# PV with three fp16 products for all four heads of a group, the fourth split by ScalarE and VectorE

## The reference

```python
h = jnp.maximum(_layernorm(x), 0.0)
q, k, v = (split_heads(h @ W.T) for W in (Wq, Wk, Wv))   # 16 heads, hd = 32
a = einsum('bhnd,bhmd->bhnm', q, k) * 512 ** -0.5 + (adj + adj)[:, None]
p = softmax(where(any(a != 0, -1, keepdims=True), a, -inf)); p = where(isnan(p), 0, p)
o = einsum('bhnm,bhmd->bhnd', p, v)
out = x + o.transpose(0, 2, 1, 3).reshape(B, N, D) @ Wo.T
```

## Time and profile before

| | |
|---|---|
| median of 3 runs | 1099.92 us (1098.54 to 1100.93) |
| profiled execution | 1103.56 us, of which the span from first to last instruction is 1101.7 us |
| mean granted TensorE clock | 0.990 |
| PE busy | 1071.4 us, 97% of the span |
| ACT busy | 923.4 us, 84% |
| DVE busy | 896.1 us, 81% |
| POOL busy | 743.8 us, 68% |
| PV: fp32 products (L1020), 512 records | 135.4 us |
| PV: fp16 products (L1025), 2304 records | 95.2 + 75.3 us |
| DVE's copy of the turned head (L720), 128 | 88.2 us |
| ACT's v_y (L541), 64 | 17.4 us |

### The profile page before, as it was taken

How to read it: one execution, slowest core, us unless ns; L and a number is a source line. 1 busy time by engine, 2 the same in 40 slices (tenths; PEclk the granted TensorE clock), 3 DMA queues, 4 the chain that set the end, 5 groups by cost and what they waited for, 6 DMA issues and landing times.

```text
span 1101.7 us, 34625 instructions
## 1 busy us (share of the span) xinstructions
PE 1071.4 (97%) x11852; PEld 716.0 (65%) x11852; DVE 896.1 (81%) x3218; ACT 923.4 (84%) x3089; POOL 743.8 (68%) x936
## 2 busy tenths in 40 slices
PE   6789999999999999999999999999999999999987
PEld 5556666666766666666666766666766666666643
DVE  6778888888888888888888888888888888888784
ACT  3488888888888888888888888888988888888884
POOL 1266776677767677677667777667776766767665
PEclk9899999999999999999999999999999999999998
DMA  6167887766777776788877788877777868777866
GB/s 229 39 116 144 161 169 150 159 142 148 156 170 160 150 151 141 153 164 167 146 159 145 153 155 166 156 152 145 150 156 167 159 149 164 133 152 140 139 124 143
DMA packets 443118, 165.84 MB, mean 151 GB/s; under 512 B 408128, under 2 KB 416320, under 8 KB 442944
## 3 DMA queue, kind: packets, MB, share of 16 engines
q1 hardware_dynamic: 442944, 163.64, 73.0%
HBM read 46.14 MB, written 16.78 MB: 57 GB/s over the span
## 4 chain that ended last, share of the span: by engine, by line
PE 93%; DVE 2%; POOL 1%; ACT 1%; DMA 1%; issue 1%; POOLq 0%; SPq 0%; DVEq 0%; ACTq 0%
PE ps L955 60%; PE ps L973 9%; PE ps L1025 6%; PE ps L1020 6%; PE ps L986 5%; PE ps L999 4%; PE ps L838 3%; DVE w_max L603 1%; POOL p L400 1%; DMA w_nat<-in_L_gnn_Wq 1%; ACT probs L492 1%; PE ps L1036 1%; PE ps L850 0%; DMA pt<-p 0%; DVE w_lo L643 0%
## 5 line engine op out<-in xcount | busy, mean ns | idle before, releaser
L400 POOL TENSOR_TENSOR p<-probs,p 128x512 f16<-128x512 f32 x384 | 445.3, 1160 | 301.0 <-ACT p L505 301.0
L683 DVE CUSTOM_DVE_ANT_0 logits<-ps,adj_s,sigma 128x256 f32<-128x256 f32 x1024 | 433.3, 479 | 102.7 <-PE ps L973 102.7
L492 ACT ACTIVATE probs<-logits,row_min 128x256 f32<-128x256 f32 x1024 | 506.3, 500 | 1.2 <-DVE row_min L683 0.7
L955 PE MATMUL ps<-ht_hi,w_hi 128*128 128x256 f16 x1024 | 280.4, 274 | 1.6 <-DVE q_lo L736 1.2
L955 PE MATMUL ps<-ht_hi,w_lo 128*128 128x256 f16 x1024 | 279.7, 273 | 0.0
L955 PE MATMUL ps<-ht_lo,w_hi 128*128 128x256 f16 x1024 | 279.7, 273 | 0.0
L505 ACT ACTIVATE p<-probs 128x512 f16<-128x512 f32 x384 | 237.6, 619 | 0.0
L492 ACT ACTIVATION_READ_ACCUMULATOR probs<-logits,row_min 128x1 f32 x1024 | 198.2, 194 | 0.0
L1020 PE MATMUL ps<-probs_t,v_y 128*32 128x256 f32 x512 | 135.4, 387 | 0.0
L955 PEld LDWEIGHTS ps<-ht_hi,w_hi 128*128 128x128 f16 x1024 | 100.3, 98 | 37.0 <-issue 25.3
L720 DVE COPY probs_t<-ps 128x512 f32<-128x512 f32 x128 | 88.2, 689 | 32.5 <-PE ps L986 32.3
(11 more groups left out here) (90 smaller groups left out, 1943.2 us busy)
## 6 DMA issues: line engine op xcount, KB each, us to landing
xs<-in_x SPq DMA_DIRECT2D x32, 512.0 KB, 4.0
x_res<-in_x SPq DMA_DIRECT2D x32, 512.0 KB, 3.9
out<-x_res SPq DMA_DIRECT2D x64, 256.0 KB, 2.4
adj_raw<-in_adj SPq DMA_DIRECT2D x32, 256.0 KB, 4.3
pt<-p SPq DMA_TRANSPOSE x384, 3.1
w_nat<-in_L_gnn_Wq SPq DMA_DIRECT2D x1, 1024.0 KB, 6.0
w_nat<-in_L_gnn_Wk SPq DMA_DIRECT2D x1, 1024.0 KB, 8.3
w_nat<-in_L_gnn_Wv SPq DMA_DIRECT2D x1, 1024.0 KB, 10.5
```

Of the source, the lines that this page charges most:

```text
L400: g.tensor_tensor(p16[:, c % 2, k, 1], probs[:, h % 4].rearrange("p u n -> p (u n)"), p16[:, c % 2, k, 0], ALU.subtract).then_inc(p_split, 1)
L492: e = a.activation(probs[:, h % 4, u, :], logits[:, h % 4, u, :], ACT.Exp, bias=row_min[:, t.par(d), u, h:h + 1], scale=-1.0, accum_out=ro ...
L683: v.tensor_tensor_reduce(out=logits[:, h % 4, u, :], in0=ps[:, S_BANK + h % HC, N * u:N * u + N], in1=adj_s[:, t.par(d), u, :], scale=sigm ...
L955: m = mm(o, l, r, start=start, stop=stop)
```

## The change

Head j = 3 of every group is treated like the others in PV: the turned probs are kept as two fp16 parts, y_hi and y_lo, in place of the fp32 probs_t, and the product is the sum of three fp16 products with v_hi and v_lo. ACT copies y_hi out of the AUX bank, in slots 0, 4, 8 and 12 between exp_rows and round_probs. DVE, at the place of its copy, waits for y_hi_ready and subtracts y_hi from the bank to give y_lo; it then frees the bank. v_y and its two ACT copies a batch are gone. The turning by PE stays fp32.

```diff
--- before.py
+++ after.py
@@ -116,7 +116,6 @@
         k_diag = sb("k_diag", [P, NC, HC], F16)
         v_hi = sb("v_hi", [P, 2, NU, D], F16)
         v_lo = sb("v_lo", [P, 2, NU, D], F16)
-        v_y = sb("v_y", [P, 2, NU, NC, NY, HD])
         logits = sb("logits", [P, 4, NU, N])
         probs = sb("probs", [P, 4, NU, N])
         row_min = sb("row_min", [P, 2, NU, H])
@@ -127,7 +126,8 @@
         norm = sb("norm", [P, 2, NU, P])
         norm_t = sb("norm_t", [P, N])
         o_norm = sb("o_norm", [P, 2, N])
-        probs_t = sb("probs_t", [P, 2, NY, NU, N])
+        y_hi = sb("y_hi", [P, 2, NU, N], F16)
+        y_lo = sb("y_lo", [P, 2, NU, N], F16)
         p16 = sb("p16", [P, 2, NX, 2, NU * N], F16)
         pt16 = sb("pt16", [P, 2, NX, 4 * NU, P], F16)
         o_hi = sb("o_hi", [P, 2, NC, N], F16)
@@ -180,6 +180,7 @@
         p_split = sem("p_split")
         pt16_in = [[sem(f"pt16_in{i}{k}") for k in range(NX)] for i in range(2)]
         v_hi_ready = sem("v_hi_ready")
+        y_hi_ready = sem("y_hi_ready")
         rows_tested = sem("rows_tested")
         norm_step = sem("norm_step")
         norm_ready = sem("norm_ready")
@@ -537,10 +538,13 @@
                     need(act, pv_done, NC * t.batch(d - 1))
                 a.activation(v_hi[:, t.par(d), u, :], ps[:, PJ_BANK + u, :], ACT.Copy, scale=DOWN)\
                  .then_inc(v_hi_ready, 1)
-                for k, j in enumerate(YJ):
-                    a.activation(v_y[:, t.par(d), u, :, k, :],
-                                 ps[:, PJ_BANK + u, :].rearrange("p (c j d) -> p c j d", c=NC, j=HC)[:, :, j, :],
-                                 ACT.Copy, scale=DOWN).then_inc(v_hi_ready, 1)
+            def take_probs_t(t, d, c):
+
+                act.wait_ge(aux_full, aux_after("y", t.batch(d), c))
+
+                need(act, pv_done, NC * t.batch(d) + (c - 1))
+                a.activation(y_hi[:, c % 2], ps[:, AUX_BANK, :].rearrange("p (m n) -> p m n", m=NU), ACT.Copy)\
+                 .then_inc(y_hi_ready, 1)
 
             def slot(t):
                 for s in range(H):
@@ -566,6 +570,10 @@
                         kc = s - 1 - WO_STEP
                         take_weight(3, kc, PJ_BANK + kc % 2)
                     exp_rows(t, s + 2)
+                    if s == 0 and t.prev:
+                        take_probs_t(t, -1, NC - 1)
+                    if s % 4 == 0 and s >= 4 and t.cur:
+                        take_probs_t(t, 0, s // 4 - 1)
                     round_probs(t, s + 1)
 
             run(act, slot)
@@ -714,15 +722,13 @@
 
             def take_probs_t(t, d, c):
 
-                dve.wait_ge(aux_full, aux_after("y", t.batch(d), c))
-
-                need(dve, pv_done, NC * t.batch(d) + (c - 1))
-                v.tensor_copy(probs_t[:, c % 2, 0], ps[:, AUX_BANK, :].rearrange("p (m n) -> p m n", m=NU))\
-                 .then_inc(aux_taken, 1)
+                dve.wait_ge(y_hi_ready, NC * t.batch(d) + (c + 1))
+                v.tensor_tensor(y_lo[:, c % 2], ps[:, AUX_BANK, :].rearrange("p (m n) -> p m n", m=NU),
+                                y_hi[:, c % 2], ALU.subtract).then_inc(aux_taken, 1)
 
             def take_v(t, d, u):
 
-                dve.wait_ge(v_hi_ready, (1 + NY) * (NU * t.batch(d) + u + 1))
+                dve.wait_ge(v_hi_ready, NU * t.batch(d) + u + 1)
                 v.scalar_tensor_tensor(out=v_lo[:, t.par(d), u, :], in0=ps[:, PJ_BANK + u, :], scalar=DOWN,
                                        in1=v_hi[:, t.par(d), u, :], op0=ALU.mult, op1=ALU.subtract)\
                  .then_inc(pj_taken[u], 1)
@@ -1016,14 +1022,12 @@
                     for j in range(HC):
                         o = ps[HD * j:HD * j + HD, PV_BANK, 0:N]
                         h = HC * c + j
-                        if j in YJ:
-                            m = mm(o, v_y[:, t.par(d), mh, c, YJ.index(j), :],
-                                   probs_t[:, c % 2, YJ.index(j), mh, :], start=(mh == 0), stop=(mh == NU - 1))
-                            continue
-                        k = XJ.index(j)
                         for i, (a, b) in enumerate(THREE):
-                            m = mm(o, (v_hi, v_lo)[a][:, t.par(d), mh, HD * h:HD * h + HD],
-                                   pt16[:, c % 2, k, 2 * NU * b + mh:2 * NU * b + mh + NU + 1:NU, :],
+                            if j in YJ:
+                                part = (y_hi, y_lo)[b][:, c % 2, mh, :]
+                            else:
+                                part = pt16[:, c % 2, XJ.index(j), 2 * NU * b + mh:2 * NU * b + mh + NU + 1:NU, :]
+                            m = mm(o, (v_hi, v_lo)[a][:, t.par(d), mh, HD * h:HD * h + HD], part,
                                    start=(mh == 0 and i == 0), stop=(mh == NU - 1 and i == len(THREE) - 1))
                 m.then_inc(pv_done, 1)
```

## The result

| | before | changed |
|---|---|---|
| median | 1099.77 us (4 runs) | 1107.94 us (1106.56 to 1108.36, 4 runs) |
| ratio | 1 | 1.0072 (95%: 1.0055 to 1.0090) |
| span of the profiled execution | 1101.7 us | 1106.6 us |
| batch in the middle | 32.67 us | 32.77 us |

A second set of six runs beside the experiments gave 1107.61 us, 1.0058 (1.0041 to 1.0075). Forecast were 1115 us and slower. The sign and the two places were right; the medians stand 8.2 us apart where 15 were forecast, and the batches in the middle account for only 3 of them.

A forecast was written before the change was run, and what follows sets the result against it. PE was taken to bound the kernel, helpers' order deciding its waits. Per batch -0.96 + 0.70 + 0.78 = +0.52 us, over 29 batches +15.1, made 1115 us; own range 1107 to 1121, 8 in 10 1091 to 1122.

The forecast's parts named there:

- the two places: New PE waits before the transposes of norm, about 0.7 us, and of probs, about 0.8 us, in 29 batches.
- What bounds: Whole kernel: PE never waits in a middle batch, busy 32.67 of 32.67 us; ACT has 4.2 us free, DVE 5.5.
- the order argument: Engines work in written order, so what counts is how long before PE's need the last helper is done.
- PV block: PV on PE: six fp16 products for the fourth head shorten each block from 1.01 to 0.77 us, 0.96 a batch.
- ACT and DVE terms: ACT gains 1.64 us a batch and still fits; DVE's subtraction lasts as long as its copy but waits for ACT.
- Chain A: From y of c = 3 in slot 0 to turn_norm in slot 5: logits 0.81 us later, PE waits 0.70 us.
- Chain B: From y of c = 1 in slot 8 to turn_probs in slot 12: late ht_lo makes PE wait 0.78 us.
- The margin before the residual: DVE's residual at 596.11 stood 0.43 us later than DVE could have done it, leaving 0.63 of 1.06 us delay.
- Sum: The waits add: a batch goes from 32.67 to 33.19 us, +0.52, over 29 batches +15.1 us.
- Ends: First batch about 0, last but one keeps -0.96 us, last batch some +1.1 us.

The follow-up runs named there:

- e3: Changed kernel with ACT's y_hi copy of c = 3 moved ahead of the exps of its slot: 1104.02 us, 1.0016 of the kernel before.
- e4: Changed kernel with ACT's y_hi copy of c = 1 moved ahead of the exps of its slot: 1085.55 us, 0.9856 of the kernel before.
- e7: Changed kernel with one more ACT copy a batch, after the exps of slot 12: 1107.78 us, 1.0050 of the kernel before.
- e8: Changed kernel with one more ACT copy a batch, in slot 7: 1122.01 us, 1.0182 of the kernel before.
- e5: Changed kernel with y_hi ahead of the exps of its slot for c = 3, 0 and 1: 1084.73 us, 0.9845 of the kernel before.
- e10: Changed kernel with only DVE's mean and variance moved from slot 2 to slot 1: 1096.64 us, 0.9968 of the kernel before.
- e9: Changed kernel with y_hi early for c = 3, 0 and 1, and mean and variance in slot 1: 1077.64 us, 0.9781 of the kernel before.
- e1: Changed kernel without the fourth head's low part: DVE copies to fp16, no y_hi on ACT (computes something else): 1075.75 us, 0.9758 of the kernel before.
- e11: Changed kernel run again unedited, as reference: 1107.61 us, 1.0058 of the kernel before.
- e6: As e5, with neg_mean written as a scalar_tensor_tensor against the changed kernel's tensor_scalar: 1083.69 us, 0.9834 of the kernel before.

## Why the prediction was right, and too high

**What bounds, and the order argument: right.** Work that fits ACT's 4.2 free us and DVE's at equal duration still cost PE 0.98 us a batch. e3, e4, e7 and e8 show that the place decides and not the amount.

**PV block.** 0.79 us in place of 0.77: 0.88 saved a batch, forecast 0.96. The fourth head's products start 0.03 us after the others' (576.26, 576.81), which the prediction had left out and which may be the 0.02 us.

**ACT and DVE terms: right.** y_hi 1.48 us after v_hi (forecast 1.47), the subtraction 0.69 us (its bounds of 0.2 us either way rested on no row), the logits 3.30 us after v_hi (forecast 3.34).

**Chain A: the term that failed.** Forecast 0.70 us of wait, measured 0.29. The prediction shifted the whole stretch from the logits to var_s by the 0.81 us of the logits. But in the kernel before that stretch held a wait for POOL's split, inside neg_mean:

```profile
580.23 1.16 POOL L400 TENSOR_TENSOR p<-probs,p 128x512 f16<-128x512 f32 x1
...
580.89 0.52 DVE L596 TENSOR_SCALAR neg_mean<-mean_var 128x2 f32<-128x2 f32 x1
```

In the changed kernel neg_mean takes 0.17 us, as it begins only 0.06 us before the split ends (584.52, 584.58). So 0.35 us of the delay was absorbed; another 0.04 came from the logits (3.30 in place of 3.34) and 0.02 from the PV block, which is the 0.41. e3 and e5 show the hold coming back, with a mean of 0.77 and 0.79 us, when the logits are early again, e10 that A leads through here alone. The prediction also left out that y_hi stands ahead of the rounding that feeds the split: the split ends 6.06 us after v_hi in place of 5.74. That cost nothing here, as e9 and e10 show, but it leaves no slack behind it.

**Chain B: right.** Forecast 0.78, measured 0.69; ht_lo ended 603.08 - 591.14 = 11.94 us after ht_hi's start, by the prediction 600.25 - 588.21 = 12.04, and PE started 0.15 us after it (0.14 forecast). (The margin before the residual comes to 0.42 us, not 0.43.) e4 confirms it: 0.71 us a batch off.

**Sum.** -0.88 + 0.29 + 0.69 = +0.10 a batch in place of -0.96 + 0.70 + 0.78 = +0.52: over 29 batches 3 us in place of 15. A small difference of larger terms: an error of 0.4 us in one of three terms of 0.7 to 1 us takes four fifths of the sum. That the sign held is in part luck: 0.10 us was left of it, and one more error of that size would have turned it.

**Ends.** Forecast about 0 together; measured +1.9 us of span. The first two batches cost some 1.6 us, where chain B in the first was put at nothing on balance. The first scores of the second batch came at 78.0 us in the kernel before and 78.1 in e1, at 79.9 here and 80.3 in e11, the same code. The wait of PE that grew most there is one that the prediction did not name, ahead of turning a weight (first row before, second changed):

```profile
69.04 0.66 PE L876 MATMUL ps<-ident,w_nat 128*128 128x128 f32 x4 [1.27 <-DVE k_lo L736]
69.61 0.66 PE L882 MATMUL ps<-ident,w_nat 128*128 128x128 f32 x4 [3.47 <-DVE k_lo L742]
```

k_lo stands behind y_lo of c = 1 on DVE; this wait is 2.5 us in e4, with that y_hi early, and 1.4 in e1. The ht_lo wait of the earlier trace rows went from 2.21 to 2.43 us. The mean granted clock from 66 to 84 us is lower too: 0.81 in the changed kernel and in e11, where this wait is 3.5 us, and 0.91 in the kernel before, e1 and e4, where it is 1.3 to 2.5. How the 1.6 us divide between these stays open. The last but one gave 0.9 us (0.96 forecast) and the end after it cost 1.2 (1.1 forecast).

**The total.** The trace accounts for 4.9 us, 3.0 in the middle and 1.9 at the ends. The other 3.3 of the 8.2 us between the medians are there because the profiled execution of before stood 3.8 us above its median and that of the changed kernel 0.4; no trace shows where they lie. The forecast's own range, 1107 to 1121, holds 1107.94 at its very edge thanks to them: that too is luck. (The page of the kernel before shows PE at nine tenths from the fourth to the 38th slice, not from the third to the 39th; nothing here rests on it.)

## What to carry to other kernels

With every engine in a hand-written order, price an added step by following it from an instruction that already waits for the bottleneck, down the engines, to the next thing the bottleneck needs; here spare busy time told nothing. Put the first half of a two-engine hand-over ahead of its engine's bulk work: here moving three calls and one small block turned +0.7% into -2.2%. Before shifting a stretch of rows rigidly, look for instructions in it that last much longer than their size asks for: they hide a wait that may shrink or grow when the stretch moves.

## What the runs showed of the hardware

An instruction of two elements per partition on DVE took 0.17 us with no POOL instruction beside it, and up to 0.86 us when it began inside POOL's 1.16 us subtraction, ending 0.01 to 0.04 us after POOL's end, as tensor_scalar (before, e1, e3, e5) and as scalar_tensor_tensor with a second SBUF operand (e6). Six rounds of four fp16 products on four column groups kept the same 0.11 us step whether their operands came from a DMA and DVE (e1) or from a DMA, ACT and DVE (changed kernel).
